# Normalised rows made by ScalarE, and gates multiplied into the output projections' weights by GpSimd

## The reference

```python
def _ln(x):
    m = x.mean(-1, keepdims=True)
    v = jnp.mean((x - m) ** 2, axis=-1, keepdims=True)
    return (x - m) * jax.lax.rsqrt(v + EPS)

h = _ln(x) * (1 + scale) + shift          # per batch and channel
h = attention(h)                          # heads joined: 256 channels
x = x + (h @ w_out + b_out) * gate        # gate: per batch and channel
```

## Time and profile before

| | |
|---|---|
| median of three runs | 2871.01 us (2868.69 to 2883.15) |
| the profiled execution, its own time | 2869.71 us |
| its span, first to last instruction | 2868.4 us |
| busy: TensorE | 84% of the span |
| busy: VectorE | 61% |
| busy: ScalarE | 44% |
| busy: GpSimd | 13% |

### The profile page before, as it was taken

The page is one execution under the profiler, slowest core; times in us unless marked ns, Lnnn a source line. Parts: engine busy times, 40 slices in busy tenths (PEclk is TensorE's granted clock), DMA queues, the critical chain, the costliest instruction groups (busy, mean ns, idle before and its releaser), DMA issues.

```text
span 2868.4 us, 37341 instructions
## 1 busy us (share of the span) xinstructions
PE 2420.5 (84%) x13127; PEld 1239.4 (43%) x13127; DVE 1745.0 (61%) x5419; ACT 1264.1 (44%) x2410; POOL 375.5 (13%) x380
## 2 busy tenths in 40 slices
PE   6768677968997979999979999978889978899668
PEld 2455344544554544554434445432324332234335
DVE  5646856666234565557767666657676677775343
ACT  2324434433221314445525555525656626656334
POOL 3002333244010100000200010010010010010201
PEclk9889688989898979999989999989999989999879
DMA  4646231000000120000411100123110122110120
GB/s 157 170 118 201 89 114 32 17 24 6 3 8 30 67 61 12 12 23 26 143 59 57 36 16 23 45 88 98 50 32 12 67 81 75 31 26 8 55 60 15
DMA packets 151647, 161.32 MB, mean 56 GB/s; under 512 B 33471, under 2 KB 120978, under 8 KB 151196
## 3 DMA queue, kind: packets, MB, share of 16 engines
q1 hardware_dynamic: 151460, 158.94, 19.2%
HBM read 98.04 MB, written 60.19 MB: 55 GB/s over the span
## 4 chain that ended last, share of the span: by engine, by line
PE 62%; DVE 16%; issue 6%; ACT 5%; DMA 5%; POOL 4%; SPq 2%; POOLq 0%; ACTq 0%; DVEq 0%
PE bank L1125 9%; PE bank L1608 8%; PE bank L1097 7%; PE bank L1072 7%; PE bank L1629 5%; PE bank L736 3%; PE bank L1101 3%; PE bank L2082 3%; DVE max L1198 3%; DVE bank L1195 2%; PE bank L1528 2%; PE bank L2259 2%; PE bank L2084 1%; PE bank L676 1%; ACT work L1139 1%
## 5 line engine op out<-in xcount | busy, mean ns | idle before, releaser
L1139 ACT ACTIVATE work<-bank 128x512 f32<-128x512 f32 (+1 forms) x1216 | 700.7, 597 | 574.6 <-PE bank L1101 259.4
L1195 DVE CUSTOM_DVE_ANT_0 bank<-bank,weights 128x512 f32<-128x512 f32 x512 | 348.8, 703 | 197.8 <-PE bank L1072 196.4
L1198 DVE TENSOR_REDUCE max<-bank 128x1 f32<-128x512 f32 x512 | 341.3, 685 | 142.4 <-PE bank L1072 140.4
L1072 PE MATMUL bank<-k_stack,q_stack 97*128 97x512 bf16 x896 | 364.4, 410 | 70.5 <-DVE max L1198 28.6
L1097 PE MATMUL bank<-q_stack,k_stack 99*128 99x512 bf16 x896 | 345.4, 388 | 12.8 <-ACT work L1139 10.3
L1608 PE MATMUL bank<-hT,weights 128*128 128x512 f32 x512 | 268.3, 624 | 16.0 <-ACT hT L697 7.4
L1453 POOL TENSOR_TENSOR x<-x,work 128x512 f32<-128x512 f32 x64 | 82.1, 1282 | 1081.3 <-DVE work L1442 1076.9
L1101 PEld LDWEIGHTS bank<-ident_b,weights 128*128 128x128 bf16 x2048 | 159.3, 98 | 119.3 <-issue 10.3
L1072 PEld LDWEIGHTS bank<-k_stack,q_stack 97*128 97x128 bf16 x896 | 90.1, 101 | 267.8 <-DVE max L1198 99.3
L1101 PE MATMUL bank<-ident_b,weights 128*128 128x128 bf16 x2048 | 200.1, 220 | 0.0
L1629 PE MATMUL bank<-weights,work 128*128 128x256 f32 x768 | 196.5, 384 | 0.0
(11 more groups left out here) (237 smaller groups left out, 3687.2 us busy)
## 6 DMA issues: line engine op xcount, KB each, us to landing
q_stack<-parts_q SPq DMA_DIRECT2D x60, 384.0 KB, 3.9
parts_q<-parts SPq DMA_DIRECT2D x46, 384.0 KB, 2.6
k_stack<-parts_k SPq DMA_DIRECT2D x40, 384.0 KB, 4.8
weights<-parts_q SPq DMA_DIRECT2D x36, 384.0 KB, 3.7
parts_q<-parts SPq DMA_DIRECT2D x46, 256.0 KB, 2.9
parts_k<-parts SPq DMA_DIRECT2D x24, 384.0 KB, 2.5
parts_k<-parts SPq DMA_DIRECT2D x24, 256.0 KB, 2.9
weights<-in_L_e_w SPq DMA_DIRECT2D x12, 512.0 KB, 5.8
```

Source lines behind the costliest of these rows:

```text
L1072: m = pe.e.matmul(bank.ap[:, :], self.q(g)[0:MAX_ROW, h, qt * P:(qt + 1) * P], k_stacks[self.key, g].ap[0:MAX_ROW, h, half * BLK:(half + 1 ...
L1139: ac.e.activation(p.ap[0:self.nk, :], banks[self.key, "exp", g, i].ap[0:self.nk, :], ACT.Exp).then_inc(*probs.tick((self.key, g, i)))
L1195: ve.e.tensor_tensor_reduce(bank[:, :], bank[:, :], mask_bias[:, qt, half * BLK:(half + 1) * BLK], 1.0, -3.4e38, ALU.add, ALU.max, to).the ...
L1198: ve.e.tensor_reduce(to, bank[:, :], AX_X, ALU.max).then_inc(*maxima.tick((self.key, g, i)))
```

## The change

ScalarE makes the normalised rows: `z = root * x + (-mean * root)`, with root and shift as columns. VectorE makes the column `-mean * root` by one small operation for each norm. Two new buffers `gated` hold the output weights multiplied by the gate; GpSimd makes one for each gated out-projection ahead of its bias additions, once weights and rows have landed. TensorE's projection waits for it. VectorE then adds each pair of tiles straight to `x` and GpSimd's additions in these stages go. The MLPs keep their way. What waited for a row of `z` on VectorE's counter waits on ScalarE's; the diff leaves out three more lines of that kind.

```diff
@@ buffers
+        gated = slots([sb(f"gated{i}", [P, CC, C]) for i in range(2)])
@@ Norm.vector
                 ve.wait_ge(*vec[key, "root"])
-                yield
-                for t in self.tiles:
-                    z = work[key, "z", t]
-                    for f in z.free:
-                        ve.wait_ge(*f)
-                    ve.e.tensor_scalar(z.ap[:, 0:C], x[b][:, t, :], mv[b][:, t, 0:1], rstd[b][:, t:t + 1],
-                                       ALU.subtract, ALU.mult).then_inc(*vec.tick((key, "z", t)))
-                    yield
+                ve.e.scalar_tensor_tensor(out=newton[b][:, 0, lo:hi], in0=mv[b][:, lo:hi, 0], scalar=-1.0, in1=rstd[b][:, lo:hi],
+                                          op0=ALU.mult, op1=ALU.mult).then_inc(*vec.tick((key, "shift")))
+                yield
@@ Norm.tensor
-                    pe.wait_ge(*vec[key, "z", t])
+                    pe.wait_ge(*evac[key, "z", t])
@@ Norm
+            def normalize(self, ac, t):
+                b, z = self.b, work[self.key, "z", t]
+                for f in z.free:
+                    ac.wait_ge(*f)
+                ac.e.activation(z.ap[:, 0:C], x[b][:, t, :], ACT.Identity, scale=rstd[b][:, t:t + 1],
+                                bias=newton[b][:, 0, t:t + 1]).then_inc(*evac.tick((self.key, "z", t)))
+
             def scalar(self, ac):
                 b, key = self.b, self.key
-                yield from rest(self.lead + 1)
+                yield from rest(self.lead)
+                ac.wait_ge(*vec[key, "shift"])
+                self.normalize(ac, self.tiles[0])
+                yield
                 if self.mods is not None:
                     ac.wait_ge(*vec[self.mods])
                 for done, k in self.free:
                     ac.wait_ge(*done[k])
                 for t in self.tiles:
+                    if t + 1 in self.tiles:
+                        self.normalize(ac, t + 1)
...
@@ Adding.pre_add
-                    po.wait_ge(*vec[self.norm.key, "z", t])
+                    po.wait_ge(*evac[self.norm.key, "z", t])
@@ Adding
             def added(self, t):
-                return (pool_done if self.gate is not None else vec)[self.key, "x", t - t % 2]
+                return (vec if self.direct else pool_done)[self.key, "x", t - t % 2]
...
-                    left.append((vec, (self.key, "y", self.tiles[-1] - 1)))
+                    left.append((pool_done, (self.key, "gated")) if self.direct else (vec, (self.key, "y", self.tiles[-1] - 1)))
@@ Adding.add_vector
-                if self.gate is None:
+                if self.direct:
                     if self.bias is not None:
                         ve.wait_ge(*pool_done[self.key, "pre", tp + 1])
+                    else:
+                        ve.wait_ge(*evac[self.norm.key, "z", tp + 1])
                     ve.e.tensor_tensor(x[b][:, tp:tp + 2, :], x[b][:, tp:tp + 2, :], src, ALU.add).then_inc(*vec.tick((self.key, "x", tp)))
@@ OutProject
+            direct = True
...
             def pool(self, po):
+                if self.gate is not None:
+                    w = gated.take(self.r, self.key, (dense, (self.key, "all")))
+                    for f in w.free:
+                        po.wait_ge(*f)
+                    po.wait_ge(*ld_w[self.wname][self.wname])
+                    po.wait_ge(*ld_tm[self.r][self.key, "rows"])
+                    po.wait_ge(*pool_done.latest)
+                    po.e.tensor_tensor(w.ap[:, :, :], wt[self.wname][:, :, :], tmc[self.r][:, 0:1, :].to_broadcast([P, CC, C]),
+                                       ALU.mult).then_inc(*pool_done.tick((self.key, "gated")))
                 self.pre_add(po)
                 yield
-                for what, tp, i in self.steps:
-                    yield
-                    if what == "pair" and i == 1 and self.gate is not None:
-                        self.add_pool(po, tp, work[self.key, "y", tp])
@@ OutProject.project
                 w = wt[self.wname]
+                if self.gate is not None:
+                    w = gated[self.key].ap
+                    pe.wait_ge(*pool_done[self.key, "gated"])
@@ Mlp
+            direct = False
```

More of the change, by code:

```diff
@@ L1450, in add_pool @@
                 else:
-                    po.wait_ge(*vec[self.norm.key, "z", tp + 1])
+                    po.wait_ge(*evac[self.norm.key, "z", tp + 1])
                 po.wait_ge(*pool_done.latest)
@@ L1512, in tensor @@
                             bank = banks.take(self.lane.banks[n % len(self.lane.banks)], k, (vec, (self.key, "y", at)))
-                            work.take(self.lane.work[4 + n % 4], (self.key, "y", at), (pool_done, (self.key, "x", at))
-                                      ) if self.gate is not None else None
                             for f in bank.free:
@@ L1520, in tensor @@
                             m.then_inc(*dense.tick(k))
+                            dense.also((self.key, "all"), k)
                             n += 1
@@ L1550, in vector @@
                         ve.wait_ge(*dense[self.key, tp])
-                        self.add_vector(ve, tp, banks[self.key, tp], work[self.key, "y", tp] if self.gate is not None else None)
+                        self.add_vector(ve, tp, banks[self.key, tp], None)
                     yield
         class Mlp(Adding):
+            direct = False
             def __init__(self, lane, b, name, norm, gated_unit, gate, bias, row_free, blk=None, r=None):
@@ L2434, in pool @@
                     t = self.bl * TPB + tp
-                    po.wait_ge(*vec[self.norm.key, "z", t + 1])
+                    po.wait_ge(*evac[self.norm.key, "z", t + 1])
                     po.wait_ge(*vec[self.key, "out", tp])
```

## The result

The changed kernel takes 2890.21 us (median of seven runs, 2886.64 to 2898.09) against 2871.01 us. The ratio is 1.0063, 95% interval 1.0046 to 1.0079: slower by 0.6%, some 18 us. The profiled execution took 2886.64 us (span 2885.2), 16.9 us above that of before.

A forecast was written before the change was run, and what follows sets the result against it. TensorE, working 84% of the span, was taken as the bound, so the change wins only where TensorE waits for what moves. Terms -6 -1 +2 +0.5 +5 -1 +4 +2.5 +3.2 +1 +1 = +11.2 gave 2881 us, range 2850 to 2899.

The forecast's parts named there:

- A sign of being wrong: Forecast wrong if L1528 hardly waits for GpSimd, or norms beside the maxima get shorter by over 2 us each.
- the five norms beside attention's maxima: Norms before or among attention's exponentials: VectorE relieved of rows, 1.2 us won each, -6 us, bounds 0 and -8.5.
- rival B: Projections: TensorE idles until each product ends, nothing absorbs it, 27.5 us in place of 11.7; 2897 us, chance 0.20.
- Rows on ScalarE: 160 row instructions in 26 norms: -6, -1, +2 and +0.5 us, with +5 us for the extra small op.
- the stretch where ScalarE is full: At 2258 us ScalarE is busy 6.62 of 8.10 us; eight more rows cost +2 us, bounds 0 and +3.
- Rival A: 26 norms: VectorE's order is the real brake, relief gives -34 in place of -6 -1 +2; 2852 us, chance 0.27.
- rival C: Every row on ScalarE is waited for and 117 ns longer, +18.7 us in place of -4.5; 2904 us, chance 0.08.
- The rule of the Trainium skill: Running GpSimd blocks VectorE's two-port tensor_scalar, never ScalarE; L654's whole excess, 6.1 us, would go, where the sum has 1.
- The small operation: Each of 26 norms: one VectorE op behind the root, 0.2 us, ScalarE waits; +5 us, bounds 2.5 and 5.2.
- GpSimd's additions gone: Gated out-projections: GpSimd's 40 additions (51 us) go, statistics waited only 10.6 us; -1 us, bounds 0 and -6.
- The waits for products: TensorE waits before its projections: +4 us at 1894, +2.5 at 2310, +3.2 at 2683, +1 each at 702 and 809.
- Near 702 and 809 us: Late products before projections: +1 us each, bounds 0 and 3.7 near 702 us, 0 and 2.1 near 809 us.

The follow-up runs named there:

- rows_only: Kernel before with only the normalised rows moved to ScalarE, small operation included, gates as before: 2865.68 us, ratio 0.9991.
- gates_only: Kernel before with only the gated weights (products on GpSimd, VectorE adding straight to x), rows still on VectorE: 2889.71 us, ratio 1.0069.
- all_early_loads: Changed kernel with late rows of gates loaded earlier and the product near 702 us ahead of GpSimd's filling of rows of ones: 2869.62 us, ratio 0.9999.
- rows_only_early_loads: Kernel before with only the normalised rows moved to ScalarE, gates as before, and the late rows of gates loaded earlier: 2862.37 us, ratio 0.9984.
- early_gates: Changed kernel, but six gated out-projections (two picked wrongly) keep the gate on VectorE and the additions on GpSimd: 2874.73 us, ratio 1.0011.
- warm_short: Changed kernel with 13, 14, 6 and 6 overwritten matmuls filling TensorE's waits for the four late products: 2887.24 us, ratio 1.0071.

## Why the prediction was right, and where it wasn't

The signs that I had named came: VectorE 1689.9 us busy (near 1680), ScalarE 1345.6 (1354), GpSimd 341.5 (341), L672 waiting 76.7 us for ScalarE (under 86). The last came for another reason than mine: TensorE waited 91.8 us for the rows in rows_only and 71.3 us in gates_only. It is the wait for the products that takes the place of a wait for rows (near 702 us 6.83 us became 1.57), not the rows that come sooner. A sign of being wrong came too: of the five norms beside attention's maxima two got shorter by over 2 us. The measured 2890.2 us lies in the range (2850 to 2899), 9 us above the forecast (2881) and 7 under rival B (2897). The likeliest class, within 0.5%, got 0.44; the ratio's interval (+0.46 to +0.79%) lies at and over that line.

- **Rows on ScalarE** (-6, -1, +2, +0.5 and +5, in sum +0.5): -2.6, between -6.6 and +1.1. Right in sum, term by term not: laid over, the five norms beside the maxima (at 1475, 1669, 1921, 2123 and 2340 us) cost -0.7, -2.0, -2.7, +0.2 and -4.6 us in rows_only, -9.8 in all, and -10.1 in the change (the last one -4.1 to -4.9 in all ten kernels with these rows whose trace can be laid over), where I had -6 with a bound of -8.5; gates_only has -0.4. With -2.6 us for the whole that leaves some +7 us for the rest, where I had +6.5, as far as places of one execution may be set against a ratio. One more term can be seen by itself: the stretch where ScalarE is full, 2250 to 2275 us, cost +3.0 us in the change and in rows_only and nothing in gates_only, where I had +2, bounds 0 and +3. ScalarE's instruction takes 596 ns, I had 563, and seven in a row 3.55 us (0.51 us each; I had 0.45 to 0.56):

```profile
2805.36 3.55 ACT L693 ACTIVATE work<-x,newton,rstd 128x256 f32<-128x256 f32 x7 [1.11 <-DVE newton L662]
```

  That is the trace of rows_only. Rival A (relief, -29 us) and rival C (ScalarE paces, +18.7 us) are both excluded by rows_only. The rule of the Trainium skill ("SBUF — State Buffer", "Who interferes with whom") would have given 6.1 us. The trace of before agrees with it on where the excess lies: all 13 instructions of L654 over 500 ns overlap one of GpSimd, and they are 6.0 us above the median together. What their going gave isn't shown: -2.6 us for rows_only as a whole neither show nor exclude 6.1.
- **The small operation** (+5, bounds 2.5 and 5.2): added ones cost 0.25 to 0.34 us each, with my 0.2 inside both intervals; for the single one 0 to 5 us stays open.
- **GpSimd's additions gone** (-1): nothing to be seen, all_early_loads is not under rows_only_early_loads (+4 us, -1 to +10, with the products' price in it).
- **The waits for products** (+11.7): the places were right and the lengths nearly so (6.69, 7.31, 3.50 and 3.36 us, with 11.67 near 702 and 2.33 near 809 us; I had some 7, 6 and 3 to 4), their price was not: gates_only cost +19.8 us (13.8 to 26), against my 10.7 and rival B's 26.5 for the same part. This is the term that was mis-sized. By place, gates_only in the laid-over table has +6.8, +6.3 and +6.8 us where I had +4, +2.5 and +3.2, and rival B (nothing absorbs the wait) 7.7, 6.3 and 7.7. But its waits at 1894 and 2310 us were longer than the change's (8.79 and 8.12 us). On top of the rows the price by place is lower: change less rows_only gives +3.7, +4.6 and +4.6 us, change less early_gates +4.0, +5.0 and +5.1, between mine and B's. The whole difference of change and rows_only, 20.7 us (15 to 27), is again above mine. Two things in my working made the term small. I priced the groups that move behind the wait at today's 1.03 us: at 1894 us they and their maxima took 7.0 us (1903.21 to 1910.2), not 4.8; at 2310 us 6.0, not 3.7; at 2683 us 9.24, not 7/8 of 7.82 = 6.84. That is 2.2 + 2.3 + 2.4 = 6.9 us by the trace of the change. And I took off 0.8 and 1.2 us because VectorE was behind there anyway. That the slow groups follow from the stall is shown by warm_short; that they make the difference in the total is not, since its total stayed.
- **Near 702 and 809 us** (+1 each): an 11.67 us wait cost 2.4 us (change minus rows_only, +3.8 - 1.4) or 3.4 us (gates_only), where B had 3.7, since TensorE had waited for rows right behind it before. The wait of 2.33 us near 809 us cost 0.4 or 0.8 us (stretch 800 to 830 us), where B had 2.1. A wait is worth what isn't waited for anyway. The kernel before, TensorE's time line near 702 us:

```profile
712.23 1.40 PE L676 MATMUL bank<-ident,work 128*128 128x128 f32 x4 [6.83 <-DVE work L654]
719.31 0.69 PE L676 MATMUL bank<-ident,work 128*128 128x128 f32 x2 [5.68 <-DVE work L654]
```

In the change, the rows gave back some 3 us in the stretches behind 1894 and 2310 us each (-2.9 and -3.2 in rows_only, from the norms at 1921 and 2340 us), so that it shows only +0.8 and +1.4 there; with -2.6 us for the rows and +19.8 us for the gates the sum is +17.2 against 18. That the total came out 9 us from the forecast is in part luck: the rows gave more at those norms than I had, and the waits for products cost more.

## What to carry to other kernels

Before a multiplication is moved from behind a matmul into its weights, look when the multiplier lands: the matmul then waits for what only the result had waited for, and everything behind it in TensorE's order waits too. Price a new TensorE wait at most of its length wherever the stretch is busy (here 14 to 15 us for 20.9 us of waits on top of the rows, and 19.9 us by the table for 23.6 us in gates_only), and at what is left where TensorE waits for something else just behind it. 55 us less of VectorE's work gave some 10 us at five norms beside attention's maxima and nothing in sum; 34 us less of GpSimd's gave nothing that could be seen.

## What the runs showed that I hadn't expected

The granted clock differs between executions of the same kernel, and the time with it. rows_only ran a span of 2877.3 us at a clock of 0.906 and of 2859.3 us at 0.919. Over all executions, 0.001 of clock goes with 1.4 us (correlation -0.7, taken within each kernel). It sits in single stretches. Busy time of PE, PEld, DVE, ACT and POOL, then the clock, the DMA share and GB/s; first the kernel before, then rows_only, where TensorE has nearly as many records:

```profile
2735.00:2775.00 40.00, 32.30 (x216) 14.85 (x220) 20.07 (x54) 21.40 (x38) 0.90 (x2) 0.73 0.19 48
2775.00:2800.00 25.00, 15.18 (x84) 11.02 (x76) 14.76 (x56) 3.63 (x7) 8.04 (x11) 0.81 0.07 22
```

```profile
2735.00:2775.00 40.00, 34.41 (x213) 16.18 (x213) 20.37 (x55) 17.47 (x30) 0.00 (x0) 0.59 0.17 43
2775.00:2800.00 25.00, 20.20 (x80) 11.77 (x78) 7.99 (x25) 7.88 (x14) 6.50 (x9) 0.70 0.12 29
```

The clock is 0.59 against 0.73 and 0.70 against 0.81, and TensorE is busy 7.1 us longer for 293 records against 300: that is much of rows_only's +8.0 us at the end. So a single profiled execution tells no difference under some 8 us here. The same goes for the numbers by place above, of which each is one execution.

Moving a stage of one beat also deals TensorE's work out anew: with the early loads, the stretch 1560 to 1620 us cost +8 us in both kernels that have them and 1885 to 1960 and 2305 to 2360 us gained 7 to 9 us; some 1,400 of TensorE's 13,127 records stand at another place in the order in them, so that the laying over is rough there. What a better place for these loads would give wasn't tried.
